# A gated attention and feed-forward block: 256-token chunks, seven half-size products for layer two, turns by DMA crossbar, queries stacked through DRAM

## The reference, cut to what matters

```python
# x (2, 2048, 512), ctx (2, 128, 512); 16 heads of 32; k0 (1024, 2048), k1 (2048, 2048), k2 (2048, 512) booleans
def xattn(q, ctx): ...          # multi-head attention over 128 keys, with Wq, Wk, Wv, Wo and biases
def dense(k, h): return h @ where(k, 1.0, -1.0)
def ffn(h):
    h = concatenate([h, -h], -1)
    h = relu(s0 * dense(k0, h)) * 2     # 512 -> 2048 (the two halves of k0 differ)
    h = relu(s1 * dense(k1, h)) * 2     # 2048 -> 2048
    return s2 * dense(k2, h)            # 2048 -> 512
x = x + tanh(g_xattn) * xattn(layernorm(x), ctx)
x = x + tanh(g_ffn)   * ffn(layernorm(x))
```

## Time and profile before

| | |
|---|---|
| median of three runs | 1744.14 us (1742.58 to 1744.47) |
| the profiled execution: first to last instruction | 1741.5 us |
| PE busy / weight loads | 1696.0 us / 856.0 us, 9400 of each |
| DVE busy, ACT busy, POOL busy | 659.9, 477.3, 147.3 us |
| share of the chain that ended last | PE 91%, issue 4%, DVE 3%, POOL 1%, ACT 1% |
| DMA | 55.03 MB, mean 32 GB/s |

### The profile page before, as it was taken

How to read it: one execution, slowest core, us unless ns; L and a number is a source line. 1 busy time by engine, 2 the same in 40 slices (tenths; PEclk the granted TensorE clock), 3 DMA queues, 4 the chain that set the end, 5 groups by cost and what they waited for, 6 DMA issues and landing times.

```text
span 1741.5 us, 24433 instructions
## 1 busy us (share of the span) xinstructions
PE 1696.0 (97%) x9400; PEld 856.0 (49%) x9400; DVE 659.9 (38%) x1199; ACT 477.3 (27%) x1088; POOL 147.3 (8%) x268
## 2 busy tenths in 40 slices
PE   6789999999999999999999999999999999999999
PEld 4444555445554555445554555544555455554444
DVE  4773324533345323443344432453334523343001
ACT  2723222223223222132321322223322222212000
POOL 1320002000010001100010000200001000010000
PEclk8989999999999999999999999999999999999999
DMA  8021000110001000020001100010000100001000
GB/s 305 18 65 25 13 13 24 51 25 14 12 25 59 16 23 2 25 69 17 13 1 74 25 13 13 1 73 25 13 13 25 52 23 18 8 1 49 1 0 25
DMA packets 36949, 55.03 MB, mean 32 GB/s; under 512 B 9840, under 2 KB 28272, under 8 KB 33904
## 3 DMA queue, kind: packets, MB, share of 16 engines
q1 hardware_dynamic: 36848, 53.52, 9.5%
HBM read 20.98 MB, written 8.39 MB: 17 GB/s over the span
## 4 chain that ended last, share of the span: by engine, by line
PE 91%; issue 4%; DVE 3%; POOL 1%; ACT 1%; DMA 0%; DVEq 0%; SPq 0%; POOLq 0%
PE bank L875 25%; PE bank L876 25%; PE bank L885 6%; PE bank L883 6%; PE bank L865 6%; PE bank L866 6%; PE bank L830 3%; PE bank L851 2%; PE bank L852 1%; PE bank L853 1%; PE bank L806 1%; PE bank L808 1%; PE bank L807 1%; PE bank L824 1%; PE bank L798 1%
## 5 line engine op out<-in xcount | busy, mean ns | idle before, releaser
L876 PE MATMUL bank<-H,W 128*128 128x512 f16 x2048 | 776.2, 379 | 0.0
L875 PE MATMUL bank<-H,W 128*128 128x512 f16 x2048 | 776.2, 379 | 0.0
L875 PEld LDWEIGHTS bank<-H,W 128*128 128x128 fp8e5 x2048 | 200.3, 98 | 218.8 <-issue 2.8
L876 PEld LDWEIGHTS bank<-H,W 128*128 128x128 fp8e5 x2048 | 200.4, 98 | 217.2
L462 ACT ACTIVATE Pf<-bank,nmax 128x128 f32<-128x128 f32 x512 | 145.9, 369 | 385.6 <-DVE nmax L594 385.6
L639 DVE SCALAR_TENSOR_TENSOR h_lo<-bank,h_hi 128x512 f16<-128x512 f32 x128 | 88.4, 691 | 358.0 <-ACT h_hi L488 358.0
L865 PE MATMUL bank<-hT,W 128*128 128x512 f16 x512 | 195.2, 381 | 10.6 <-issue 7.3
L866 PE MATMUL bank<-hT,W 128*128 128x512 f16 x512 | 195.0, 381 | 0.0
L885 PE MATMUL bank<-W,h_lo 128*128 128x512 fp8e5 x512 | 194.0, 379 | 0.0
L883 PE MATMUL bank<-W,h_hi 128*128 128x512 fp8e5 x512 | 194.0, 379 | 0.0
L488 ACT ACTIVATE h_hi<-bank 128x512 f16<-128x512 f32 x128 | 76.8, 600 | 383.6 <-PE bank L876 383.6
(11 more groups left out here) (100 smaller groups left out, 1426.3 us busy)
## 6 DMA issues: line engine op xcount, KB each, us to landing
Qst<-Qhl SPq DMA_DIRECT2D x448, 32.0 KB, 1.9
Y<-in_x_dram SPq DMA_DIRECT2D x8, 1024.0 KB, 4.8
XR<-XR SPq DMA_DIRECT2D x8, 1024.0 KB, 4.7
out_dram<-XR SPq DMA_DIRECT2D x7, 1024.0 KB, 5.3
H<-in_L_ffn_k_dram SPq DMA_DIRECT2D x1, 4096.0 KB, 20.0
W<-in_L_xattn_Wk_dram SPq DMA_DIRECT2D x1, 1024.0 KB, 6.3
W<-in_L_xattn_Wq_dram SPq DMA_DIRECT2D x1, 1024.0 KB, 11.0
W<-in_L_xattn_Wv_dram SPq DMA_DIRECT2D x1, 1024.0 KB, 12.7
```

What stands on the lines that cost most here:

```text
L875: mm(banks[n % 2][:, :], w, h0_hi[:, k, :], start=k == 0, stop=False)
L876: last = mm(banks[n % 2][:, :], w, h0_lo[:, k, :], start=False, stop=k == FT - 1)
```

## The change

The chunk is 256 tokens and there are 16 of them, so a chunk has U = 8 units, and 14 chunks run in the two loops, with 12 jumps back.

L1 becomes one level of a Winograd form of Strassen's product. The weight is cut into 2 by 2 blocks and the chunk's tokens into an early and a late half of 128; instead of eight products of half-size blocks there are seven (STEPS), with weight sums that are made once and kept in fp8, and activation sums that are made for each pair of L0 tiles. Per group q (of four) and step there are 32 matmuls of 128 columns. The results are joined by ACT (`take`) and DVE (`add`), and the parts of h1 are written from there.

L0 works on pairs of tiles. ACT writes both tiles' relu to Fp as f32, DVE makes the four sums from them in three instructions, ACT writes the high parts of seven blocks (896 columns), DVE the remainders. Fp has two buffers: the relu of pair n waits for the remainders of pair n - 2.

All turns leave PE. What was T1, T, CT and T2 on PE becomes: ACT writes the high part and DVE the remainder, untransposed, to xs or Phl, and SP issues one DMA_TRANSPOSE of 128 by 1024 f16 (256 KB) for both parts. SP issues 14 of them per chunk (2 for T1, 8 for the units as item PS, 2 for CT, 2 for T2).

Query stacking goes through DRAM: item QS writes Qhl with two copies to q_bounce, item QL reads them back with two copies into Qst. Two slots "L2P" after the last L0 slot do the last group of L2 of the chunk before. The four groups of weight sums take five DVE instructions each: the first group ahead of chunk 0's feed-forward part, the others within it (LATE_WEIGHTS).

```diff
-    CHUNK = 512
+    CHUNK = 256
-    SLOTS = [("L0", n, 0) for n in range(FT)]
-    for n in range(FT):
-        SLOTS += [("L1", n, 0), ("L1", n, 1)] + ([("L2", n - 1, 0)] if 0 < n < FT - 1 else [])
-        SLOTS += [("L1", n, 2), ("L1", n, 3)]
-    SLOTS += [("L2", FT - 2, 0), ("L2", FT - 1, 0)]
+    STEPS = [(A_L11, B_R11, A, True), (A_L12, B_R21, B, True), (A_S2, B_T2, A, False),
+             (A_S1, B_T1, C, True), (A_S3, B_T3, A, False), (A_L22, B_T4, A, False),
+             (A_S4, B_R22, C, False)]
+    P1, P2, P6, P5, P7, P4, P3 = range(7)
+    SLOTS = [("L0", i, 0) for i in range(PAIRS)] + [("L2P", GROUPS - 1, h) for h in range(2)]
+    for q in range(GROUPS):
+        SLOTS += [("L1", q, s) for s in (P1, P2, P6, P5, P7)]
+        SLOTS += [("L2", q - 1, h) for h in range(2)] if q else []
+        SLOTS += [("L1", q, s) for s in (P4, P3)]
...
+    for t in range(TT):
+        weave(2 + t, "T1", t)
+    for g, slot in enumerate((6, 9, 14, 19)):
+        weave(slot, "Q", g)
+        weave(slot, "QS", g)
+        weave(slot + 1, "QL", g)
+    for u in range(U):
+        weave(10 + 5 * u // 2, "S", u)
+        weave(11 + 5 * u // 2, "PS", u)
+        weave(15 + 5 * u // 2, "PV", u)
+    for t in range(TT):
+        weave(32 + 2 * t, "CT", t)
+        weave(35 + 2 * t, "WO", t)
...
+                    wait_apart(sp, xs_lo, nth(a, NX, k))
...
+                    sp.dma_start_transpose(dst[:, :, n * P:(n + 1) * P],
+                                           xs[:, k % 2].rearrange("p h d -> p (h d)"))\
+                      .then_inc(crossed[k % 2], 16)
...
+                if kind == "QS":
+                    wait_apart(sp, q_lo, nth(a, NG, n))
...
+                    for hl in range(2):
+                        sp.dma_start(q_dram[n, hl].rearrange("d j q -> j d q"), Qhl[:, n % 2, hl, :])\
+                          .then_inc(q_kept[n % 2], 16)
...
+                    for r in range(2):
+                        sp.dma_start(Qst[64 * r:64 * r + 64, n % 2, :, :].rearrange("p j q -> p (j q)"),
+                                     q_dram[n].rearrange("h d j q -> (h d) (j q)"))\
+                          .then_inc(q_stacked[n % 2], 16)
...
+                if kind == "L0":
+                    act.wait_ge(l0_done, nth(f, NP, n))
+                    if n >= 2:
+                        act.wait_ge(l0_lo, nth(f, NP, n - 2))
...
+                    nc.scalar.activation(Fp[:, n % 2, 0:4, :],
+                                         banks[n % 3][:, :].rearrange("p (b n) -> p b n", b=4), ACT.Relu)\
+                        .then_inc(l0_relu, 1)
+                    if n >= 1:
+                        pair_hi(n - 1, f, once)
...
+            def pair_lo(i, f):
+                dve.wait_ge(l0_hi, nth(f, NP, i))
+                V_.tensor_tensor(H0[:, 1, i], Fp[:, i % 2, 1:8, :], H0[:, 0, i], ALU.subtract).then_inc(l0_lo, 1)
...
+                if kind == "L0":
+                    Fi = Fp[:, n % 2]
+                    dve.wait_ge(l0_relu, nth(f, NP, n))
+                    V_.tensor_tensor(Fi[:, 4:6, :], Fi[:, 1:3, :], Fi[:, 0:1, :].to_broadcast([P, 2, HALF]),
+                                     ALU.subtract).then_inc(l0_step, 1)
...
+                    V_.tensor_tensor(Fi[:, 6, :], Fi[:, 5, :], Fi[:, 1, :], ALU.add).then_inc(l0_step, 1)
...
+                    V_.tensor_tensor(Fi[:, 7, :], Fi[:, 3, :], Fi[:, 6, :], ALU.subtract).then_inc(l0_t, 1)
+                    if n >= 1:
+                        pair_lo(n - 1, f)
...
+                    if n >= 3:
+                        wait_apart(pe, l0_relu, nth(f, NP, n - 3))
...
+                    for i in range(PAIRS):
+                        if s == P1 and n == 0:
+                            wait_apart(pe, l0_lo, nth(f, NP, i))
+                        for j in range(2):
+                            o = banks[bank][:, j * HALF:(j + 1) * HALF]
+                            w = W1[:, n, a_of, i, j * P:(j + 1) * P]
+                            first = opens and i == 0 and j == 0
+                            mm(o, w, H0[:, 0, i, b_of, :], start=first, stop=False, skip_group_check=True)
+                            last = mm(o, w, H0[:, 1, i, b_of, :], start=False, stop=i == PAIRS - 1,
+                                      skip_group_check=True)
```

More of the change, by code:

```diff
@@ L89, in gated_block_kernel @@
-    LOOP_ITEMS = [item for slot in sorted(WEAVE) for item in WEAVE[slot]]
[L94 to L107, removed]
@@ L490, in _ @@
-            for item in ACT_FIRST_ITEMS:
+                if kind == "PS":
+                    act.wait_ge(p_ready, nth(a, NU, n))
+                    if n >= 2:
+                        act.wait_ge(p_crossed[n % 2], nth_half(a, NU, n - 2))
+                    elif not first:
+                        act.wait_ge(p_crossed[n % 2], nth_half(a - 1, NU, n + NU - 2))
+                    nc.scalar.activation(Phl[:, n % 2, 0, :], Pf[:, n % 2, :], ACT.Copy, scale=PS)\
+                        .then_inc(p_hi, 1)
@@ new lines, in pair_hi, with take @@
+            def pair_hi(i, f, once):
+                act.wait_ge(l0_t, nth(f, NP, i))
+                if i == 0 and not once:
+                    act.wait_ge(l1_done, nth(f - 1, NL1, NL1 - 1))
+                nc.scalar.activation(H0[:, 0, i], Fp[:, i % 2, 1:8, :], ACT.Copy).then_inc(l0_hi, 1)
+            def take(q, s, f, to, bank):
+                act.wait_ge(l1_done, nth(f, NL1, 7 * q + s))
+                nc.scalar.activation(to[:, :, :], banks[bank][:, 0:CHUNK].rearrange("p (j n) -> p j n", j=2),
+                                     ACT.Copy).then_inc(l1_copy, 1)
@@ L491, in _ @@
+            for item in FIRST_ITEMS:
                 prepare(item)
-                attend(item, 0, first=True)
+                attend(item, 0, True)
             for s, slot in enumerate(SLOTS):
-                if slot[0] == "L0" and slot[1] % 2 == 0:
-                    act.wait_ge(w1_made, slot[1] + 2)
-                feed(slot, 0)
+                feed(slot, 0, True)
                 for item in WEAVE.get(s, ()):
-                    attend(item, 1, second=True)
+                    attend(item, 1)
@@ L783, in attend @@
                     return
[L784 to L789 removed]
+                items, of = (FIRST_ITEMS, FIRST_BANK) if first else (LOOP_ITEMS, LOOP_BANK)
@@ L790, in attend @@
+                before, since = user_before(items, of, item), a
+                if before is None and not (first or second):
+                    before, since = [i for i in items if of.get(i) == of[item]][-1], a - 1
                 if before is not None:
-                    signal, per_chunk, m = released(before, a)
+                    signal, per_chunk, m = released(before)
                     pe.wait_ge(signal, nth(since, per_chunk, m))
-                bank = banks[bank]
-                if kind in ("T1", "T2"):
-                    k = n + (TT if kind == "T2" else 0)
-                    pe.wait_ge(xn_ready, nth(a, NX, k))
-                    for d in range(KT):
-                        last = turn(bank[:, d * P:(d + 1) * P], xn[:, k % 2, d * P:(d + 1) * P],
-                                    ident[:, :])
-                    last.then_inc(xn_turned, 1)
+                bank = banks[of[item]]
```

773 lines of the change are left out of this document (436 added, 337 removed).

## The result

| | before | changed |
|---|---|---|
| median | 1744.31 us (1742.58 to 1746.50, 4 runs) | 1813.59 us (1812.27 to 1815.14, 4 runs) |
| span of the profiled execution | 1741.5 us | 1813.3 us |

The ratio is 1.0398, with an interval from 1.0383 to 1.0413. The change is slower, as forecast, but by 4.0% where the prediction had 0.9%.

What follows compares the result with a forecast made beforehand. PE's own stream, busy 97% of the span, was taken as the bound. Prologue 108 + chunk 0 118 + 14 x 102.6 + last chunk 95 = 1757, with 2.6 around it 1760 us, 0.9% slower; eight-in-ten range 1695 to 1850.

Steps and rivals of the forecast that it cites:

- PE's work: PE's matmuls and turns: 206.9 us per 512 tokens fall to 184.2, with L1's 128-column products at 0.0555 us each.
- The rival with the weight loads as bound: L1: if weight loads could not overlap, matmuls cost 0.098 us each, 609 us more, some 2370 us; chance 0.03.
- L0's round: L0's relu, sums and remainders with two Fp buffers: 2.9 us per pair, against 1.75 us on PE.
- X: Time from DVE's remainder to the landed DMA turn: taken as 3.6 us, bounded by 2.6 and 6.6.
- The long turns: Rival on DMA turns: X of 5.5 to 6.6 us makes chunks of 109 to 113, 1855 to 1910 us; chance 0.16.
- the cheaper DVE: Rival on DVE's SBUF work: L0's round 2.4 us, chunk 98.4, total 1685; chance 0.35 for all faster outcomes.
- The jump: Jump back of the loops: 1.8 us each, 12 over 14 chunks, 1.5 us per chunk.
- The prologue: Work before the first L0 product: 108 us, from 98 to 118, against 110.9 in the kernel before.
- The stacking of queries: Q's trip through DRAM: 5.3 us within the 5.7 that Q(0) leaves before S(0), costed at nothing.
- Chunk 0: First chunk, with three more groups of weight sums on DVE: 15 us more, 118 us.
- the last chunk: Final chunk, without attention: 26.5 us for L0, 64.5 for the rest of L1 and L2, 4 for the end: 95.
- The 2.6 us around the span: Time outside the profiled span, added to the forecast span of 1757 us to give 1760.

Runs made afterwards that it cites:

- e3: Changed kernel, loops kept, with a third Fp buffer for a pair's relu and sums, on PT's memory: 1793.30 us, ratio 1.028 to the kernel before.
- e7: Changed kernel with loops written out, a third Fp buffer, and N1 and T1 one slot earlier for the second token tile: 1706.32 us, ratio 0.978.
- e6: Changed kernel with loops written out and eight products instead of seven, without sums of weights or activations: 1714.09 us, ratio 0.982.
- e8: e1 with 36 idle matmuls of 256 columns ahead of Q(0)'s wait for the turned tokens: 1750.01 us, ratio 1.003.
- e10: Kernel before with its loops written out and nothing else: 1736.09 us, ratio 0.995.
- e1: Changed kernel with its two loops written out, nothing else: 1744.21 us, ratio 1.000 to the kernel before.
- e5: e3 with Q(0) and its stacking items one slot later, behind the eighth pair of L0, loops kept: 1826.44 us, ratio 1.048.
- e9: e6 with N1 and T1 one slot earlier for the second token tile: 1712.77 us, ratio 0.982.
- e12: e7 with T1's turns ahead of K's write and k1 loaded by POOL after Q(1)'s stack landed: 1700.55 us, ratio 0.974.
- e11: e9 with T1's turns ahead of K's write and k1 loaded by POOL after Q(1)'s stack landed: 1707.03 us, ratio 0.978.
- e2: Changed kernel, loops kept, with POOL instead of ACT issuing the k1 loads: 1806.30 us, ratio 1.036.

## Why the prediction was right or wrong

- **PE's work** was right: 0.055 us for a 128-column product in a long stream. The rival with the weight loads as bound is refuted, and the 81 ns of the Trainium skill (*TensorE: Matmul & The Clock Gate*, Back-to-back issue gap) do not hold here. The loads overlap, at 73% of the span.
- **L0's round** was right in mechanism and price: 2.80 for 2.9, DVE 1085 ns for 1.09 us, ACT 943 ns for 0.90. That Q(0) came at 19.1 for 18.5 in the chunk shown was in part luck: without a jump in front it is 16.9, and L1 starts at 26.4 for 28.1. A chunk without jumps takes 99.8 us for 101.1, so over 14 chunks the sum was 18 us too high here. e3 showed that the buffers bound the stage, e7 that DVE's order holds a part of Q(0), and e6 that the seven products bring the stage's waits.
- **X** was right: 3.3 us in most chunks and 3.8 in the one shown, for 3.6, and a turn of 256 KB itself lands in 3.1 us. The Trainium skill's rule (*Advanced Engine Details and Errata*, X-Bar Transpose) that it goes like a copy agrees in the main: 128 KB by plain copy from DRAM take 2.7 us. Only beside a large load is it 12.2 us. The long turns and the cheaper DVE are both refuted.
- **The jump**, "1.8 x 12/14 for the jump back", is the first term that failed. The jumps cost 71 us instead of 21.6. I took a row of the old body for one that holds in any, but PE stands idle for about 6.2 us (first loop) or 3.2 us (second) behind a jump of the new body, and then some 1.6 us more go to the low clock. The prediction itself prices a gap's clock at 1.8 us, for the gap at Q(0) (e8 has 1.7), and left it out for the gap at the jump. e10 confirms the row for the old body, e1 the cost in the new.
- **The prologue**, "I take 108", is the second: 136.5, beyond its own bound of 118. I summed DVE's rounds, but neither SP's issue of K's scattered write (8.0 us, with T1's turns behind it) nor ACT's issue of the k1 loads (24.5 us) nor the load's effect on what else is in flight was in the sum. The weight sums that were in it cost 1 us there, by e6.
- **The stacking of queries**, costed at nothing, cost nearly nothing (12.3 us of waits, 6.3 of them in one wait), so the number held but the reason did not: e5 and e8 show that it had no slack.
- Chunk 0 and the last chunk were right within 4 us. The 2.6 us around the span are 1.8 (1815.14 against 1813.3 in the profiled execution).

The jumps were priced 50 us too low and the prologue 28.5; the chunk without a jump was priced 18 too high in all, and chunk 0 and the last chunk 4.5. That makes the 56 us by which the span came out longer. The direction was luck in this sense: with the jumps and the prologue as priced, and all else as measured, the span would have been 1735 us, under the 1741.5 of the kernel before. It was the two failed terms that made the change slower, and not the gap and the clock in L0 alone, which the prediction named.

## What to carry to other kernels

A price is only as good as the body that it was read in: what a jump back or a DMA issue costs must be read, or bounded, for the new instruction stream, and every issuing engine of the prologue belongs in the sum. When a stage's gap is closed, ask which path stands next behind the same point; here the stacked queries arrived within about half a microsecond of their use. Moving Q(0) and filling the gap in front of it only moved the idle time behind it, where the clock fell as well, and both made the kernel slower; only moving the start of the whole chain (T1) paid. Price a new gap twice, as idle time and as what the clock does behind it, and ask whether the stage behind it can bear that. The saved eighth of the products paid off only after its sums had a third buffer and T1 came sooner: with two buffers it cost 30 us (e1 against e6), mended it gains 6.5 (e7 against e9, and e12 against e11).

## What the runs showed of the hardware

- A jump back cost 1.8 us in the kernel before. In the changed one PE stood idle for 5.8 to 6.4 us behind each jump of the first loop and 2.9 to 3.5 us in the second, though the bodies are alike. The first loop's gaps had two 16 KB reads of instructions in them and the second's one.
- The granted clock was 0.50 to 0.68 over the first 3.6 us behind these gaps (0.53 in the chunk shown) and 1.00 behind the 1.8 us of the kernel before. Behind waits of 1.3 to 2.6 us at S(0) in e8 it fell in 6 chunks of 14.
- ACT needed 1.8 to 3.9 us for the issue of one 512 KB load of k1 (15.79 for four, 7.09 for three), POOL 1.2 us (8.20 us for seven in e12). SP needed 8.0 us for K's two scattered writes in the changed kernel, 15.9 in e2 beside the loads of k1, and 4.6 in e12 behind T1's turns.
- With a 4.2 MB load in flight, a 256 KB turn and a 128 KB copy took 12.2 and 12.3 us to land instead of 3.1 and 2.7.
